# The quantised feed-forward layer at the end of an eight-sublayer transformer kernel, rewritten as one block and begun in the attention before it

## The chip, the core and the metric

The kernel runs on one core of one Trainium2 chip. The metric is the device time of one execution in microseconds (us); lower is better. TensorE is the matrix engine, VectorE (DVE), ScalarE (ACT) and GpSimd (POOL) are the three elementwise engines, SyncE (SP) issues the DMAs here.

## The reference

Activations x are 16 sequences of 256 tokens of 128 numbers, 4096 tokens in all, float32. Four pairs of sublayers follow, each `x = x + attention(layernorm(x))` and then `x = x + ffn(layernorm(x))`. The change is in the last feed-forward layer, with some of its work moved into the fourth attention (layer number 3, which the change's name calls the third). The last layer is this:

```python
def act_qdq(x):                      # 16 bits, one scale for the whole tensor
    scale = max(max(abs(x)) / 32767, 1e-12)
    return clip(round(x / scale), -32768, 32767) * scale
def fixed_qdq_u16(x):                # steps of 1/65536
    return clip(round(x * 65536), 0, 65535) / 65536
def lpbq_dequant(w): ...             # 4 bits, one scale for each block of 32 weights
x = act_qdq(x)
up = act_qdq(x @ lpbq_dequant(w_up).T)          # w_up, w_gate: 384 x 128
gate = act_qdq(x @ lpbq_dequant(w_gate).T)
gate = act_qdq(gate * fixed_qdq_u16(sigmoid(gate)))
o = act_qdq(gate * up)
return o @ lpbq_dequant(w_down).T
```

Each `act_qdq` needs the largest magnitude of a whole tensor before its first element can be quantised. So the layer is five passes over its data with a hard stop between each two: X (the normalised input), G (gate), U (up), GS (gate times its sigmoid) and O (the product).

## The kernel before

x stays in SBUF as `x_sb`, 128 partitions by 32 tiles of 128 numbers. Work goes in ITERS = 8 groups of four tiles, 512 tokens each. One program is written out for each engine and block, with named semaphores; an engine runs its list in order, and between two blocks all engines meet at a barrier. Nothing else sets the order.

**The attention before the last layer** (`narrow_attention`, layer 3, lines 608 to 1079) runs over b = 0 to 15. In step b VectorE adds the projection of sequence b-2, takes four row maxima of sequence b+1 (`largest`, L1012), and normalises the heads of sequence b-1 (`normalise`, L1019 and L1021), which TensorE projects in its next step. GpSimd adds biases and takes the roots of the layernorms; its last work is for group 7. The raw weights of the last layer (`wraw`, 128x1152) are loaded during this attention.

**The last layer** (`layer3_ffn`, L2136 to L2447) has five blocks.

1. *Normalise and transpose.* VectorE takes the statistics of all 32 tiles (L203), quantises the weights in seven steps over 128x1152 (L2230 to L2236) and normalises four tiles at a time (L2248), each followed by a row maximum (`largest`, L2240). GpSimd takes the roots (L232). TensorE transposes weights and x, ScalarE copies both out of PSUM.
2. *Project.* VectorE quantises a group of x (L2294, L2297), TensorE makes six 128x512 products (L2276; the trace counts two instructions for each float32 product), ScalarE copies them out (L2288), VectorE takes maxima over 1536 columns (L2302).
3. *Gate.* 24 rows of 512 columns go through ScalarE (L2338, L2340, L2345 the sigmoid), VectorE (L2354 to L2369) and a product on GpSimd (L2327), four rows deep.
4. *Product.* 24 rows: ScalarE L2387, VectorE L2395 and L2399.
5. *Down.* ScalarE L2428 and VectorE L2438 quantise a group of 1536 columns, TensorE multiplies it with the down weights (L2417), VectorE adds it to x (L2443).

At each of the five maxima `scale_vector` (L2175 to L2184) reduces to one column, GpSimd takes the maximum over partitions (L2188), and four short VectorE instructions make scale and inverse. After block 5 one DMA stores all of x (L2514).

Rounding is by adding and subtracting `MAGIC` = 1.5 * 2**23. On VectorE block 3 is this, for row r:

```python
nc.vector.tensor_scalar(gq[:, k, :], gq[:, k, :], -MAGIC, None, ALU.add)               # L2354
nc.vector.tensor_scalar(sg, sg, 65536.0, 65535.0, ALU.mult, ALU.min)                   # L2359
nc.vector.tensor_reduce(am[:, GS, bass.ds(r - 3, 1)], part(gtf, r - 3), ...)           # L2362
nc.vector.tensor_scalar(part(upf, r - 1), uq[:, (k - 1) % DEPTH, :], -MAGIC, None, ALU.add)
nc.vector.tensor_scalar(sg, sg, MAGIC, -MAGIC, ALU.add, ALU.add)                       # L2369
```

## Time and profile before

| | us |
|---|---|
| median of 3 runs | 1825.35 (1823.53 to 1826.36) |
| the profiled execution: device time | 1827.8 |
| its span, first to last instruction | 1826.0 |
| last layer, 1592.2 to 1826.0 | 233.8 |
| granted TensorE clock, mean | 0.924 of full speed |

The five blocks of the last layer begin at 1592.2, 1622.3, 1672.9, 1757.2 and 1789.4 us, and the last addition to x ends at 1819.06. A profile tells for each instruction its start, its length and what its engine waited for before it. The lengths of neighbours on one engine overlap by some 0.08 us, so that a row of equal instructions advances by a little less than the length of one. The granted clock is the share of 2.4 GHz that TensorE is given: 0.5 is 1.2 GHz.

### The profile page before, as it was taken

The numbers are of one execution on the slowest core, as the hardware profiler recorded it, in microseconds if no ns is written. First come the engines' busy times: TensorE is split into PE (matmuls) and PEld (weight loads), VectorE is DVE, ScalarE is ACT, GpSimd is POOL, SyncE is SP. The second block draws the span as 40 slices with busy tenths as digits, with TensorE's granted clock in tenths as the row PEclk, the third lists the DMA queues.
The fourth block names the chain that finished last, engine by engine and source line by source line (L and its number), as shares of the span: only waits on it lengthen the run. The fifth ranks groups of instructions, "written<-read, shape, count | busy, mean of one in ns | idle before, by whom it ended". The sixth has DMA issues, their size and how long they took to land. (4 is left out here: it accounts for less than half of the span.)

```text
span 1826.0 us, 25615 instructions
## 1 busy us (share of the span) xinstructions
PE 1502.6 (82%) x8105; PEld 1027.9 (56%) x8125; DVE 1257.8 (69%) x2784; ACT 886.6 (49%) x1622; POOL 201.7 (11%) x191
## 2 busy tenths in 40 slices
PE   6999988886999999889848999999999888665005
PEld 5777765554666666566536665666667455432005
DVE  3988965875677766566646666666665578677984
ACT  3666545773665555555513223322332267447742
POOL 2111012130000000211310000000000111011410
PEclk9999998997999999999969999999999999878557
DMA  4000003220000000332122234423443122000001
GB/s 164 1 1 0 1 1 97 68 53 1 1 1 1 0 0 1 99 102 57 29 93 116 112 120 162 162 107 124 162 162 133 56 60 53 19 0 0 0 0 46
DMA packets 32700, 108.01 MB, mean 59 GB/s; under 512 B 8845, under 2 KB 12301, under 8 KB 23502
## 3 DMA queue, kind: packets, MB, share of 16 engines
q1 hardware_dynamic: 32590, 106.64, 17.3%
q8 instruction: 57, 0.93, 0.2%
q14 instruction: 53, 0.43, 0.1%
HBM read 85.38 MB, written 2.36 MB: 48 GB/s over the span
## 5 line engine op out<-in xcount | busy, mean ns | idle before, releaser
L1012 DVE TENSOR_REDUCE mP_a<-psY_a 128x8 f32<-128x512 f32 x192 | 128.1, 688 | 101.1 <-PE psY_a L838 101.0
L756 ACT ACTIVATE probs_a<-psX_a 128x512 f32<-128x512 f32 x192 | 109.0, 595 | 125.1 <-PE psX_a L865 124.3
L1797 ACT ACTIVATE xsh_f<-xs_f 128x512 fp32r<-128x512 f32 x128 | 79.4, 630 | 166.9 <-DVE xs_f L2025 166.9
L2417 PE MATMUL ps_f<-wT_f,xq_f 128*128 128x128 f32 x192 | 26.0, 300 | 125.4 <-DVE xq_f L2438 125.3
L1555 DVE SCALAR_TENSOR_TENSOR g_f<-psU_f,cols_f1w,t_f 128x512 f32<-128x512 f32 (+1 forms) x104 | 78.0, 750 | 72.6 <-ACT t_f L1368 70.6
L1901 PE MATMUL psX_f<-xs_f,wo_f2w 128*128 128x512 f32 x256 | 121.3, 606 | 2.1 <-DVE xs_f L2025 1.5
L1368 ACT ACTIVATE t_f<-psU_f,cols_f1w 128x512 f32<-128x512 f32 (+1 forms) x104 | 71.2, 684 | 76.1 <-PE psU_f L1434 76.1
L1450 PE MATMUL psO_f<-h_f,w_f1w 128*128 128x512 f32 (+1 forms) x208 | 107.6, 599 | 0.0
L2029 DVE TENSOR_TENSOR xsl_f<-xs_f,xsh_f 128x512 fp32r<-128x512 f32 x128 | 87.9, 687 | 16.0 <-ACT xsh_f L1797 14.9
L838 PE MATMUL psY_a<-ks_a,xs_a 96*128 96x256 f32 x384 | 94.4, 347 | 4.1 <-DMA xs_a<-ql_a 2.5
L865 PE MATMUL psX_a<-xs_a,ks_a 128*128 128x256 f32 x384 | 86.1, 324 | 13.3 <-ACT xs_a L745 13.3
L2417 PEld LDWEIGHTS ps_f<-wT_f,xq_f 128*128 128x128 f32 x192 | 24.8, 212 | 127.2 <-issue 126.8
L1019 DVE RECIPROCAL heads_a<-psV_a 128x256 f32<-128x256 f32 x48 | 84.0, 1749 | 12.6 <-PE psV_a L878 12.6
L1913 PE MATMUL psQ_f<-xsh_f,wql_f2w 128*128 128x512 f32 x128 | 58.7, 459 | 35.2 <-DVE xsl_f L2029 34.8
L838 PEld LDWEIGHTS psY_a<-ks_a,xs_a 96*128 96x128 f32 x384 | 64.0, 198 | 33.9 <-DVE mP_a L1012 22.6
L182 POOL TENSOR_TENSOR rstd_f<-vareps_f,mhalf 128x4 f32<-128x4 f32 x16 | 18.1, 1133 | 562.0 <-DVE vareps_f L168 562.0
L1562 DVE TENSOR_TENSOR h_f<-act_h_f,psR_f 128x512 f32<-128x512 f32 (+1 forms) x104 | 70.6, 678 | 13.7 <-ACT act_h_f L1374 8.8
L865 PEld LDWEIGHTS psX_a<-xs_a,ks_a 128*128 128x128 f32 x384 | 63.3, 195 | 28.1 <-ACT xs_a L745 24.6
L1901 PEld LDWEIGHTS psX_f<-xs_f,wo_f2w 128*128 128x128 f32 x256 | 45.0, 192 | 48.9 <-issue 29.9
L1374 ACT ACTIVATE act_h_f<-g_f 128x512 f32<-128x512 f32 (+1 forms) x104 | 65.0, 625 | 3.2 <-DVE g_f L1555 3.0
L468 PE MATMUL psC_a<-vhat_a,pT_a 128*128 128x128 f32 x512 | 63.5, 278 | 0.5 <-DVE x_sb L545 0.5
L468 PEld LDWEIGHTS psC_a<-vhat_a,pT_a 128*128 128x128 f32 x512 | 61.5, 195 | 1.4 <-issue 0.6
(441 smaller groups left out, 4006.6 us busy)
## 6 DMA issues: line engine op xcount, KB each, us to landing
wq_f2w<-f_routes SPq DMA_DIRECT2D x16, 1024.0 KB, 4.7
wk_f2w<-f_routes SPq DMA_DIRECT2D x16, 1024.0 KB, 4.7
wv_f2w<-f_routes SPq DMA_DIRECT2D x16, 1024.0 KB, 4.6
ring_f2w<-f_routes SPq DMA_DIRECT2D x16, 1024.0 KB, 4.6
xs_a<-qh_a SPq DMA_DIRECT2D x168, 64.0 KB, 2.0
xs_a<-ql_a SPq DMA_DIRECT2D x84, 64.0 KB, 2.0
xs_a<-probs_a SPq DMA_DIRECT2D x36, 64.0 KB, 2.0
x_sb<-in_x SPq DMA_DIRECT2D x1, 2048.0 KB, 8.4
```

The source lines that it names most:

```text
L468: ins = nc.tensor.matmul(psC[:, 0:P], pT[:, g % 2, k * P:(k + 1) * P], vhat[:, g // TPI % 2, g % TPI // 2, k, :], start=k == 0, stop=k == ...
L756: nc.scalar.activation(probs[:, b % 2, g, :, :], psX[g % 2][:].rearrange("p (e t) -> p e t", e=2), ACT.Exp, scale=float(dv) ** -0.5).then_ ...
L838: ins = nc.tensor.matmul(psY[h % 2][:, e * GK:(e + 1) * GK], xs[0:MAXROW, j % 2, g, t:t + P], ks[0:MAXROW, j % 2, p, g, :], start=not mask ...
L865: ins = nc.tensor.matmul(psX[g % 2][:, e * ST:(e + 1) * ST], ks[:, j % 2, p, g, e * P:(e + 1) * P], xs[:, j % 2, g, p * ST:(p + 1) * ST], ...
L1012: nc.vector.tensor_reduce(mP[:, b % 2, h // 2, col:col + 8], psY[h % 2][:].rearrange("p (h k) -> p h k", h=8), axis=AX.X, op=ALU.max).then ...
L1019: nc.vector.reciprocal(heads[:, b % 2, :], psV[:, ST:2 * ST]).then_inc(s("sums_inverted").sem, 1)
L1368: nc.scalar.activation(t3[r, g % 2, :], psU[g % 2][r, 1, :], ACT.Identity, bias=cols[r, CH + g % CH:CH + g % CH + 1])\
L1450: ins = nc.tensor.matmul(psO[:], w2[0:rows[k], k, :], h[0:rows[k], g % 2, :], start=False, stop=k == CH - 1)
L1555: nc.vector.scalar_tensor_tensor(g_[r, g % 2, :], psU[g % 2][r, 0, :], cols[r, k:k + 1], t3[r, g % 2, :], ALU.add, ALU.mult).then_inc(s("h ...
L1797: nc.scalar.activation(xsh[:, e % RING, :], xs[:, e % RING, :], ACT.Copy).then_inc(s("x_high").sem, 1)
L1901: nc.tensor.matmul(psX[:], wo[:, e, :], xs[:, e % RING, :], start=e == 0, stop=e == E - 1)\
L2029: nc.vector.tensor_tensor(xsl[:, e % RING, :], xs[:, e % RING, :], xsh[:, e % RING, :], ALU.subtract)\
```

## The change

Work is moved out of block 1 into the attention's last steps: VectorE makes the weight scales at b = 11, the statistics of the first 16 tiles at b = 15 and their variances after that; GpSimd rounds the weights (four instructions over 1152 columns) and takes the roots for those 16 tiles. The five blocks become one, with no barrier inside. In it ScalarE normalises groups 0 to 3 and VectorE groups 4 to 7; TensorE runs filling matmuls (`keep_busy`) whose result nobody reads; the inverse of G is made as soon as the last gate maximum is there, ahead of the last maximum of U. Gate and product go in 8 operations of 1536 columns in place of 24 of 512. The sigmoid is clipped and rounded to 1/65536 by one instruction (adding 192), and a VectorE instruction takes 192 off and multiplies; GpSimd multiplies nothing. The rounding of up moves from VectorE to ScalarE. Each group of x is stored by a DMA of its own as soon as it is added to. The diff, cut to its core (project, down and the addition to x keep their instructions):

```diff
             ahead.split(pr, pool)
+            if layer == 3:
+                f3_weight_integers(pr, pool, ahead.tensors)
+                f3_rstd(pr, pool, common, ahead.tensors, 0)
...
                 if p and j + 2 < ITERS:
                     front_q(j + 2)
+                if layer == 3 and b == B - 5:
+                    dve.wait_ge(s("ahead").sem, s("ahead").at(16 * len(ahead.loads)))
+                    f3_weight_scales(pr, dve, ahead.tensors)
+                if layer == 3 and b == B - 1:
+                    f3_stats(pr, x_sb, ahead.tensors, range(HALF))
                 if b:
                     normalise(b - 1)
...
             add(B - 2)
+            if layer == 3:
+                f3_variances(pr, dve, Steps(dve, s("dve_steps"), ITERS, LN_STEPS), ahead.tensors, 0)
             normalise(B - 1)
             add(B - 1)
...
+def f3_weight_scales(pr, dve, t):
+    nc, done = pr.nc, pr.sig("w3_scales")
+    nc.vector.tensor_reduce(t["ws"][:], f3_blocks(t), axis=AX.X, op=ALU.max, apply_absolute_value=True).then_inc(done.sem, 1)
+    dve.wait_ge(done.sem, done.at(1))
+    nc.vector.tensor_scalar(t["ws"][:], t["ws"][:], 1.0 / 7.0, 1e-12, ALU.mult, ALU.max).then_inc(done.sem, 1)
+    dve.wait_ge(done.sem, done.at(2))
+    nc.vector.reciprocal(t["wi"][:], t["ws"][:]).then_inc(done.sem, 1)
...
+def f3_weight_integers(pr, pool, t):
+    nc, step = pr.nc, pr.sig("w3_steps")
+    wb = f3_blocks(t)
+    pool.wait_ge(pr.sig("w3_scales").sem, pr.sig("w3_scales").at(3))
+    nc.gpsimd.tensor_tensor(wb, wb, t["wi"][:].unsqueeze(2).broadcast_to(list(wb.shape)), ALU.mult).then_inc(step.sem, 1)
...
+    nc.gpsimd.tensor_scalar(t["wraw"][:], t["wraw"][:], MAGIC, -MAGIC, ALU.add, ALU.add).then_inc(step.sem, 1)
+    pool.wait_ge(step.sem, step.at(2))
+    nc.gpsimd.tensor_scalar(t["wraw"][:], t["wraw"][:], 7.0, -8.0, ALU.min, ALU.max).then_inc(step.sem, 1)
...
+def f3_rstd(pr, pool, w, t, half):
+    pool.wait_ge(pr.sig("var_half").sem, pr.sig("var_half").at(1))
+    for part in range(2):
+        a = half * HALF + part * HALF // 2
+        c = slice(a, a + HALF // 2)
+        pr.nc.gpsimd.tensor_tensor(t["rstd"][:, c], t["vareps"][:, c], w["mhalf"][:, 0:HALF // 2], ALU.pow)\
+            .then_inc(pr.sig("rstd_half").sem, 1)
...
+            @block.sync
+            def _(sp):
+                for i in range(ITERS):
+                    sp.wait_ge(s("x_added").sem, s("x_added").at(i + 1))
+                    sp.dma_start(out[:, i * TPI:(i + 1) * TPI, :], tile4(x_sb, i)).then_inc(s("out_stored").sem, 16)
...
+                nc.gpsimd.memset(magic[:], MAGIC).then_inc(s("pool_steps").sem, 1)
+                nc.gpsimd.memset(unmagic[:], -MAGIC).then_inc(s("pool_steps").sem, 1)
+                f3_rstd(pr, pool, common, wt, 1)
+                for n, k in enumerate((X, G, U, GS, O)):
+                    pool.wait_ge(s("absmax").sem, s("absmax").at(n + 1))
+                    nc.gpsimd.partition_all_reduce(gm[:, k:k + 1], amr[:, k:k + 1], P, bass.bass_isa.ReduceOp.max)\
...
+                def keep_busy(n):
+                    for _ in range(n):
+                        nc.tensor.matmul(PS[4][:], sel[:, 0, :], sel[:, 0:4, :], start=True, stop=True)
                 for k in range(3):
                     for j in range(NI):
                         ins = nc.tensor.transpose(PS[5 + k][:, j * P:(j + 1) * P], wraw[:, k, j * P:(j + 1) * P], ident[:])
                     ins.then_inc(s("vT").sem, 1)
+                keep_busy(8)
                 for i in range(ITERS):
-                    pe.wait_ge(s("ln_out").sem, s("ln_out").at(i + 1))
-                    pe.wait_ge(s("xT_ready").sem, s("xT_ready").at(i - 1))
+                    if i < ITERS // 2:
+                        pe.wait_ge(s("xn_act").sem, s("xn_act").at(i + 1))
+                    else:
+                        pe.wait_ge(s("xn_dve").sem, s("xn_dve").at(i + 1 - ITERS // 2))
+                    pe.wait_ge(s("xT_ready").sem, s("xT_ready").at(max(0, i - 3)))
                     for c in range(TPI):
-                        ins = nc.tensor.transpose(PS[i % 2][:, c * P:(c + 1) * P], xq[:, i % 2, 0, c * P:(c + 1) * P], ident[:])
+                        ins = nc.tensor.transpose(PS[i % 4][:, c * P:(c + 1) * P], xn(i)[:, c * P:(c + 1) * P], ident[:])
                     ins.then_inc(s("ln_T").sem, 1)
+                    keep_busy(12 if i == ITERS - 1 else 4)
...
+                pe.wait_ge(s("hidden_b").sem, s("hidden_b").at(ITERS * NP))
+                pe.wait_ge(s("o_made").sem, s("o_made").at(ITERS - 1))
+                keep_busy(28)
...
+                nc.scalar.activation(junk[:], magic[:], ACT.Sigmoid, scale=0.0)
+                def normalised(i):
+                    act.wait_ge(s("nb_ready").sem, s("nb_ready").at(1))
...
+                normalised(0)
+                normalised(1)
+                keep_x(0)
+                normalised(2)
+                keep_x(1)
+                normalised(3)
+                keep_x(2)
+                for k in range(3):
+                    keep_w(k)
+                for i in range(3, ITERS):
+                    keep_x(i)
...
+                scales(2)
+                gate_scaled(0)
+                gate_scaled(1)
+                for r in range(ITERS):
+                    sigmoid(r)
+                    if 1 <= r < ITERS - 1:
+                        gate_scaled(r + 1)
+                    up_scaled(r)
+                for r in range(3):
+                    up_int(r)
+                scales(4)
+                for r in range(ITERS):
+                    product_scaled(r)
+                    if r + 3 < ITERS:
+                        up_int(r + 3)
+                scales(5)
+                for r in range(ITERS):
+                    out_scaled(r)
...
+                nc.vector.scalar_tensor_tensor(nb[:], mean[:, 0:HALF], -1.0, rstd[:, 0:HALF], ALU.mult, ALU.mult)\
+                    .then_inc(s("nb_ready").sem, 1)
+                f3_stats(pr, x_sb, wt, range(HALF, TILES))
+                f3_variances(pr, dve, st, wt, 1)
+                for i in range(3):
+                    dve.wait_ge(s("xn_act").sem, s("xn_act").at(i + 1))
+                    largest(X, i, xn(i))
...
+                dve.wait_ge(s("maxed").sem, s("maxed").at(3 * ITERS - 1))
+                inverse(G, 2)
+                def gate_int(r):
+                    dve.wait_ge(s("scaled").sem, s("scaled").at(r + 1))
+                    nc.vector.tensor_scalar(qb[:, r % 2, :], qb[:, r % 2, :], -MAGIC, None, ALU.add).then_inc(s("gate_int").sem, 1)
+                def gated(r):
+                    dve.wait_ge(s("hidden_act").sem, s("hidden_act").at(r + 1))
+                    sg = sig[:, r % 2, :]
+                    nc.vector.tensor_scalar(sg, sg, 65535.0 / 65536.0, ROUND16, ALU.min, ALU.add).then_inc(s("hidden_ready").sem, 1)
+                    dve.wait_ge(s("hidden_ready").sem, s("hidden_ready").at(r + 1))
+                    nc.vector.scalar_tensor_tensor(gt[:, r, :], sg, -ROUND16, qb[:, r % 2, :], ALU.add, ALU.mult)\
+                        .then_inc(s("gated").sem, 1)
...
+                largest(U, ITERS - 1, up[:, ITERS - 1, :])
+                gate_int(0)
+                all_maxed(3)
+                inverse(U, 3)
+                for r in range(ITERS):
+                    gated(r)
+                    if r + 1 < ITERS:
+                        gate_int(r + 1)
+                    dve.wait_ge(s("gated").sem, s("gated").at(r + 1))
+                    largest(GS, r, gt[:, r, :])
+                all_maxed(4)
+                inverse(GS, 4, scale[:, G:G + 1])
...
+                def out_product(r):
+                    dve.wait_ge(s("gs_scaled").sem, s("gs_scaled").at(r + 1))
+                    dve.wait_ge(s("up_ready").sem, s("up_ready").at(r + 1))
+                    nc.vector.scalar_tensor_tensor(gt[:, r, :], gt[:, r, :], -MAGIC, up[:, r, :], ALU.add, ALU.mult)\
+                        .then_inc(s("o_made").sem, 1)
+                for r in range(ITERS):
+                    out_product(r)
+                    if r:
+                        dve.wait_ge(s("o_made").sem, s("o_made").at(r))
+                        largest(O, r - 1, gt[:, r - 1, :])
...
```

The order of instructions on VectorE in the attention, step b = 11. `heads_a` is what `normalise` makes, `x_sb` the addition. Before:

```order
L1004 SCALAR_TENSOR_TENSOR ql_a<-psF_a,cols_a3w,qh_a 128x512
L1019 RECIPROCAL heads_a<-psV_a 128x256
L1021 TENSOR_TENSOR heads_a<-psV_a,heads_a 128x256
L1028 TENSOR_TENSOR x_sb<-x_sb,psT_a 128x256
L1012 TENSOR_REDUCE mP_a<-psY_a 128x8 x4
```

And now:

```order
L1008 SCALAR_TENSOR_TENSOR ql_a<-psF_a,cols_a3w,qh_a 128x512
L2162 TENSOR_REDUCE ws_f3w<-wraw_f3w 128x36
L2164 TENSOR_SCALAR ws_f3w<-ws_f3w 128x36
L2166 RECIPROCAL wi_f3w<-ws_f3w 128x36
L1023 RECIPROCAL heads_a<-psV_a 128x256
L1025 TENSOR_TENSOR heads_a<-psV_a,heads_a 128x256
L1032 TENSOR_TENSOR x_sb<-x_sb,psT_a 128x256
L1016 TENSOR_REDUCE mP_a<-psY_a 128x8 x4
```

Three instructions of the weight scales stand between the query part of group 7 and the normalisation of sequence 10.

VectorE at the attention's end, from the addition of sequence 13. Before (the last three rows are normalisation and addition of sequence 15):

```order
L1028 TENSOR_TENSOR x_sb<-x_sb,psT_a 128x256
L1019 RECIPROCAL heads_a<-psV_a 128x256
L1021 TENSOR_TENSOR heads_a<-psV_a,heads_a 128x256
L1028 TENSOR_TENSOR x_sb<-x_sb,psT_a 128x256
L1019 RECIPROCAL heads_a<-psV_a 128x256
L1021 TENSOR_TENSOR heads_a<-psV_a,heads_a 128x256
L1028 TENSOR_TENSOR x_sb<-x_sb,psT_a 128x256
```

And now, from right behind that addition:

```order
L2185 BN_STATS stats_f3w<-x_sb 128x6 x16
L1023 RECIPROCAL heads_a<-psV_a 128x256
L1025 TENSOR_TENSOR heads_a<-psV_a,heads_a 128x256
L1032 TENSOR_TENSOR x_sb<-x_sb,psT_a 128x256
L2194 TENSOR_TENSOR mv_f3w<-stats_f3w 128x16
L2195 SCALAR_TENSOR_TENSOR mv_f3w<-stats_f3w 128x16
L2196 TENSOR_TENSOR mv_f3w<-stats_f3w 128x16
L2197 TENSOR_SCALAR mean_f3w<-mv_f3w 128x16
L2198 SCALAR_TENSOR_TENSOR mv_f3w<-mv_f3w 128x16
L2199 SCALAR_TENSOR_TENSOR vareps_f3w<-mv_f3w 128x16
L1023 RECIPROCAL heads_a<-psV_a 128x256
L1025 TENSOR_TENSOR heads_a<-psV_a,heads_a 128x256
```

Sixteen statistics stand ahead of the normalisation of sequence 14, six short instructions ahead of that of sequence 15.

VectorE in the gate pass, one round. Before, for one of 24 rows (address arithmetic left out):

```order
L2354 TENSOR_SCALAR xT_f<-xT_f 128x512
L2359 TENSOR_SCALAR xT_f<-xT_f 128x512
L2362 TENSOR_REDUCE am_f<-gt_f 128x1
L2366 TENSOR_SCALAR up_f<-xq_f 128x512
L2369 TENSOR_SCALAR xT_f<-xT_f 128x512
```

And now, for one of 8 (and the first of the next):

```order
L2474 TENSOR_SCALAR xT_f<-xT_f 128x1536
L2476 SCALAR_TENSOR_TENSOR gt_f<-xT_f,qb_f 128x1536
L2469 TENSOR_SCALAR qb_f<-qb_f 128x1536
L2412 TENSOR_REDUCE am_f<-gt_f 128x1
L2474 TENSOR_SCALAR xT_f<-xT_f 128x1536
```

A round has four instructions of 1536 columns where three rows had fifteen of 512.

## Rows read from the trace of the kernel before

**Rows 1.** busy time by stage of the last layer: stretch, length, five engines, TensorE clock, DMA
```profile
1592.00:1623.40 31.40, 9.71 (x41) 7.25 (x42) 28.62 (x93) 6.25 (x11) 8.15 (x7) 0.55 0.00 0
1623.40:1672.80 49.40, 43.49 (x96) 18.95 (x96) 35.14 (x40) 32.99 (x48) 0.70 (x2) 0.95 0.00 0
1672.80:1757.20 84.40, 0.00 (x0) 0.00 (x0) 72.71 (x126) 54.26 (x73) 31.80 (x25) 0.50 0.00 0
1757.20:1789.40 32.20, 0.00 (x0) 0.00 (x0) 29.93 (x54) 17.02 (x24) 0.35 (x1) 0.50 0.00 0
1789.40:1819.10 29.70, 25.96 (x192) 24.80 (x192) 13.69 (x16) 13.23 (x8) 0.00 (x0) 0.85 0.00 0
1819.10:1826.00 6.90, 0.00 (x0) 0.00 (x0) 0.00 (x0) 0.00 (x0) 0.00 (x0) 0.72 0.72 304
```

**Rows 2.** VectorE timeline, attention of layer 3: start, length, instruction, idle before it
```profile
1582.99 1.76 DVE L1019 RECIPROCAL heads_a<-psV_a 128x256 f32<-128x256 f32 x1 [3.21 <-PE psV_a L878]
...
1587.91 1.76 DVE L1019 RECIPROCAL heads_a<-psV_a 128x256 f32<-128x256 f32 x1 [1.47 <-PE psV_a L878]
```

**Rows 3.** VectorE timeline, last layer
```profile
1592.20 6.29 DVE L203 BATCH_NORM_STATS2 stats_f<-x_sb 128x6 f32<-128x128 f32 x32 [0.32 <-PEq L616]
...
1599.43 1.34 DVE L2230 TENSOR_REDUCE ws_f<-wraw_f3w 128x36 f32<-128x1152 f32 x1
...
1601.03 0.38 DVE L2232 RECIPROCAL wi_f<-ws_f 128x36 f32<-128x36 f32 x1
...
1605.70 2.14 DVE L2248 TENSOR_SCALAR xq_f<-x_sb,mean_f,rstd_f 128x128 f32<-128x128 f32 x8
...
1620.31 0.16 DVE L2178 TENSOR_REDUCE amr_f<-am_f 128x1 f32<-128x8 f32 x1
...
1712.72 1.52 DVE L2359 TENSOR_SCALAR xT_f<-xT_f 128x512 f32<-128x512 f32 x1
```

**Rows 4.** GpSimd timeline, last layer
```profile
1599.67 7.61 POOL L232 TENSOR_TENSOR rstd_f<-vareps_f,mhalf_f 128x8 f32<-128x8 f32 x4 [7.35 <-DVE vareps_f L212]
...
1755.30 0.38 POOL L2188 PARTITION_ALL_REDUCE gm_f<-amr_f  x1 [5.98 <-issue]
```

**Rows 5.** groups by line of the last 286 us: instruction, count, busy us, mean ns
```profile
L2438 DVE TENSOR_SCALAR xq_f<-xq_f 128x1536 f32<-128x1536 f32 x8 | 7.7, 960 | 8.5 <-ACT xq_f L2428 8.5
...
L2302 DVE TENSOR_REDUCE am_f<-gt_f (+1 forms) x8 | 14.0, 1752 | 6.3 <-ACT gt_f L2288 6.0 <-issue 0.2
...
L2395 DVE SCALAR_TENSOR_TENSOR gt_f<-gt_f,up_f (+1 forms) x24 | 16.4, 684 | 1.5 <-ACT gt_f L2387 1.5
...
L2428 ACT ACTIVATE xq_f<-gt_f,magic_f,inv_f 128x1536 f32 x8 | 13.2, 1666 | 26.7 <-PEq L2379 15.2 <-PE ps_f L2417 11.6
...
L2338 ACT ACTIVATE xT_f<-gt_f,magic_f,inv_f 128x512 f32 (+1 forms) x24 | 19.5, 811 | 16.1 <-POOL gt_f L2327 10.8 <-PEq L2261 5.2
...
L2345 ACT ACTIVATE xT_f<-xT_f,scale_f 128x512 f32<-128x512 f32 x24 | 17.3, 720 | 5.8 <-DVE xT_f L2354 5.8
...
L2276 PE MATMUL ps_f<-xq_f,wT_f 128*128 128x512 f32 x96 | 43.5, 616 | 3.1 <-DVE xq_f L2297 3.1
```

**Rows 6.** GpSimd groups by form, whole span
```profile
L139 POOL TENSOR_TENSOR wkl_f2w<-wk_f2w,wkh_f2w 128x2048 fp32r<-128x2048 f32 x1 | 4.6, 4628 | 0.1
```

**Rows 7.** TensorE timeline, filling matmuls at the start of the attention of layer 3
```profile
1455.82 2.09 PE L892 MATMUL psV_a<-sel 128*128 128x512 f32 x8
```

**Rows 8.** ScalarE timeline, a copy out of PSUM in the projection
```profile
1641.26 0.69 ACT L2288 ACTIVATE up_f<-ps_f,scale_f 128x512 f32 x1 [0.17 <-PE ps_f L2276]
```

**Rows 9.** chain of waits of the last layer: start, length, what
```profile
1792.20 11.36 PE ps_f L2417 x72
...
1803.59 5.84 PE ps_f L2417 x48
```

**Rows 10.** DMA issues: KB each, median us from issue to landing
```profile
out<-x_sb SPq DMA_DIRECT2D x1, 2048.0 KB, 6.3
...
xs_a<-qh_a SPq DMA_DIRECT2D x168, 64.0 KB, 2.0
```

446 lines of the change are left out of this document (194 added, 252 removed).

## The prediction

> **What bounds the kernel now.** I read the granted clock by stage first, then the timelines of VectorE, ScalarE, GpSimd and TensorE over the last layer, then the groups by line for the price of each form. The chain of waits covers only the final block, so it doesn't help ahead of 1789 us. The change touches nothing before 1554 us; all of it happens in the last 270 us.
>
> The six stages of the last layer show who is busy [rows 1]: in the first 31.4 us VectorE for 28.6; in the projection TensorE for 43.5 of 49.4; in the gate pass VectorE for 72.7 of 84.4; in the product pass VectorE for 29.9 of 32.2; in the down pass TensorE for 26.0 of 29.7; then 6.9 us for the store. So it is VectorE, TensorE, VectorE, VectorE, TensorE, DMA, and each is followed by a stop.
>
> The gate pass costs VectorE 3.03 us a row, 72.7 us for 24. Of that, 1.44 us is one clipping instruction over 512 columns, listed at 1.52 us [rows 3]; its neighbours of the same kind and size take 0.41. It starts 0.07 us behind a GpSimd product of 1.31 us, and ends with it. The products cost VectorE 1.1 us in each row.
>
> **The change part by part.** All times of the new block are counted from its start t = 0, which is 1592.2 us of before. Prices of 1536 columns: VectorE's subtraction 0.96 us, its maximum 1.75, ScalarE's quantisation 1.67 [rows 5]. The two-operand instruction is 0.684 for 512 [rows 5], so for 1536 it is 1.75 by the slope of the maximum. The sigmoid is 0.72 for 512 [rows 5]; with ScalarE's slope of (1.666 - 0.811) / 1024 a column it is 1.57. Behind each other without a wait they advance by some 0.08 less on VectorE (1.67, 0.88) and 0.11 less on ScalarE (1.55).
>
> *Attention.* The weight scales are three dependent instructions, from 1599.43 to 1601.41 [rows 3], 2.0 us. In step b = 11 VectorE has nothing to cover them: its waits in a step are of 0.5 to 0.8 us for TensorE, and TensorE waits for VectorE's heads in the same step. Between no delay and 2.0 us I take 2.0. The 16 statistics are half of 6.29 [rows 3], 3.15 us, and stand where VectorE waited 3.21; the six short instructions, 0.9 us, stand where it waited 1.47 [rows 2]. Both cost nothing; without that cover they would cost 4.0. GpSimd's four weight instructions: at 4.63 us for 2048 columns [rows 6] one of 1152 takes 2.6, all four 10.4, from about 1557 to 1567 us, and the next work for GpSimd is at 1587.
>
> *Normalisation.* Before, TensorE began the projection 31.2 us behind the block's start. Now VectorE is through statistics and variances at t = 4.3, GpSimd's two roots end at 8.2 (7.61 for four [rows 4]). ScalarE loads its table (the 1.28 us before the first sigmoid, in the timeline), and normalises 4 x 128 columns at 0.40 each by the slope above, 1.6 us a group. TensorE turns the weights (9 transposes, 2.2 us) and fills: eight matmuls at 0.43 at half clock, up to 5.7. From then a group costs it 0.55 for four transposes and 4 x 0.24 (seven steps of (2.09 - 0.39) / 7 [rows 7]), 1.5. The first copy of x ends at 6.7, ScalarE's groups 2 and 3 at 8.3 and 10.5, VectorE's third maximum at 8.9, its group 4 at 10.0. Behind 10.5 VectorE alternates 1.1 (eight normalisations in 2.14 [rows 3]) and 0.6, up to the last maximum at 16.7. The scale takes 1.4 (1620.31 to 1621.75), the first group of quantised x 0.9: 19.0. TensorE has turned the last group at 16.8 and fills twelve times, to 19.6, which is later. Saved: 31.2 - 19.6 = **11.6**.
>
> *Projection.* 48 products; the pitch at full clock is 0.86 (a copy of 0.69 and a wait of 0.17 for the next product [rows 8]), 41.3 us against 43.5 [rows 5]. The clock was 0.95 in that stage and half at its start [rows 1]; with TensorE filling right up to it I take all of the difference: **2.2**. It ends at t = 60.9.
>
> *From the last product to the gate pass.* Before: 6.0 us (1666.9 to 1672.86), with two maxima, two scales and a barrier. Now the scale of G follows the last gate maximum, which ends 0.1 ahead of TensorE's end, so 1.4 later: t = 62.3, saved **4.6**. The last maximum of U and its scale run beside ScalarE's first two quantisations.
>
> *Gate pass.* VectorE has 0.88 + 1.67 + 0.88 + 1.67 = 5.1 a round. The chain of one round is clip and round 0.99, product 1.67, integers 0.99, sigmoid 1.61: 5.26. ScalarE has 1.55 + 1.55 + 1.57 = 4.7, so the chain decides. The first sigmoid ends at t = 67.1, eight rounds less the one missing subtraction end at 108.2, the scale at 109.7. That is 47.4 us against 83.7 (the 84.4 of [rows 1] less a barrier): **36.3**. In the 83.7 is a wait of 5.98 us by GpSimd ahead of the maximum over partitions [rows 4]; here it has nothing else to do and 0.55 us is enough, as at the first. ScalarE with its three first roundings of up is 0.3 late; the barrier of 0.67 goes: **0.4**.
>
> *Product pass.* Eight times 1.67 + 1.67, plus the first 1.7 and the scale 1.7: 30.2 against 31.45, **1.2**, and its barrier **0.7**. It ends at t = 140.2.
>
> *Down.* The first 36 products of 96 ran at half clock: 11.36 us, where the next 24 took 5.84, 2.92 for twelve [rows 9]. 28 filling matmuls start at t = 133.5 and take 8.5 to 9.3, the first at half clock, and the first group is ready at 142.9. So eight groups at 2.92: 26.9 from the stop to the last addition, against 29.65: **2.8**.
>
> *Store.* 2048 KB land in 6.3 us and 64 KB in 2.0 [rows 10], so 256 KB between; along the line 2.4. All but the last are covered. 6.9 becomes 3.1: **3.9** (bounds 0 and 4.4).
>
> Sum: 11.6 + 2.2 + 4.6 + 36.3 + 0.4 + 1.2 + 0.7 + 2.8 + 3.9 - 2.0 = 61.7. The profiled execution took 1827.8, so 1766.1; the median of the runs is 2.45 lower, which gives **1763.7**.
>
> GpSimd runs its maximum over partitions behind other work, and the trace shows what that can cost: the 5.98 us of [rows 4] come right behind its last product. At the first maximum, 1620.61, it answered in 0.14 us, 13.3 us behind its last root. Now this gap is from 8.2 to 16.9, 8.7 us, more than 5.98, so I add nothing. The Trainium skill (GPSIMD Engine Reference, 2.1 Instruction dispatch) says that the first call to freshly loaded code pays about 6 us with nothing shown. By that rule, too, the load would end at 14.2 if it begins behind the last root, and the sum stays; if it began with the call, the sum would lose 6.
>
> **The rivals.**
> 1. *TensorE stays at half clock in the normalisation.* For: it was at 0.55 there [rows 1], and it starts the block behind idle stretches. Against: 9 transposes and 8 fillings stand in one piece, and the projection reached full clock after some 4 us of unbroken work. At half clock a group costs 0.9 + 1.7 = 2.6; the last transposes end at 24.8, the fillings at 30, and nothing of 11.6 and 2.2 is left but 1.2: 1776.
> 2. *GpSimd's 5.98 us is exposed at the first maximum*, because the gap counts from the request. Against: the answer at 1620.61. 1769.7.
> 3. *A round of the gate pass is longer*, since clip, product and sigmoid wait for each other and an answer between engines may take more than the 0.04 I gave. At 6.0 us a round: 1769.6. On the other side, the weight scales may be absorbed and the product pass may start on time: 1761.
> 4. *Slower: GpSimd's rounding of the weights outlasts the attention.* The price per column in this trace is 2.3 ns for a subtraction [rows 6] but 240 ns for a root (7.61 us for 32 columns [rows 4]). From 7.5 us for each of the four instructions it delays the roots of the first half and with them the block; from 23 us each (20 ns a column) the kernel is slower than before. At the root's price it would be some 1100 us for the four: 2840. Multiplications, additions and minima are next to the subtraction and not to the root, so I give it little.
> 5. *The change doesn't do what it says*: the filling matmuls may not raise the clock for the down pass, 2.8 us: 1766.5.
>
> **How the numbers follow.** The sum as forecast 0.62 (1763.7); rival 1: 0.12; rival 2: 0.06; rival 3 with its other side 0.12; rival 5: 0.05; rival 4: 0.03, of which 0.01 is slower. The range takes in rivals 1 to 3 and 5 and, below, the bounds of scales (2.0), normalisation (ScalarE's 128 columns at 0.3, 1.5) and gate rounds at 5.1 (1.3), with as much again for what I didn't see: 1756 to 1777. The likeliest case alone is 1760 to 1768. Some 0.2%, 3.7 us, is what a measurement tells from no change. Faster 0.98, same 0.01, slower 0.01.
>
> **What would show it.** Right: the new block starts near 1594; the projection's first product some 20 us later at clock 1.0; rounds of the gate pass every 5.3 us; VectorE's clip at 0.96 us; passes of 30 and 27 us; the last DMA landing within 2.5 us. Wrong: the granted clock at 0.5 ahead of the projection (rival 1), GpSimd issuing its first maximum late (rival 2), idle VectorE in the gate pass (rival 3), or an attention that ends at 1600 or later (rival 4).

## The result and the profile after

The change takes the kernel from 1824.44 us (median of 4 runs, 1821.03 to 1826.36) to **1770.03 us** (median of 4, 1768.6 to 1771.26). The ratio is 0.9703, with a 95% interval of 0.9687 to 0.972: about 54 us, 3% faster. The profiled execution took 1769.78 us with a span of 1767.8 (before: 1827.8 and 1826.0), at a mean granted clock of 0.945 (before 0.924). The forecast was 1763.7, with 61.7 us less from one profiled execution to the other; their spans differ by 58.2.

Busy time by stage of the changed last layer, with the columns of [rows 1]: normalisation, projection, gate, product, down, store.

```profile
1597.10:1615.30 18.20, 17.72 (x90) 14.30 (x90) 15.11 (x55) 13.19 (x29) 3.74 (x5) 0.91 0.01 1
1615.30:1658.10 42.80, 41.42 (x97) 18.11 (x96) 32.35 (x35) 32.98 (x48) 0.35 (x1) 1.00 0.00 1
1658.10:1705.80 47.70, 0.00 (x0) 0.00 (x0) 45.33 (x43) 41.94 (x27) 0.70 (x2) 0.51 0.00 0
1705.80:1737.40 31.60, 8.27 (x27) 6.64 (x28) 27.90 (x23) 19.91 (x14) 0.35 (x1) 0.56 0.00 0
1737.40:1765.30 27.90, 24.71 (x195) 23.53 (x193) 13.67 (x16) 13.22 (x8) 0.00 (x0) 0.94 0.18 66
1765.30:1767.80 2.50, 0.00 (x0) 0.00 (x0) 0.02 (x1) 0.00 (x0) 0.00 (x0) 1.00 0.28 105
```

The first column against [rows 1] shows where the time went: 31.4 to 18.2, 49.4 to 42.8, 84.4 to 47.7. VectorE is busy for 45.3 of 47.7 us of the gate pass, where it was busy for 72.7 of 84.4: it is still hardly ever idle there, with the work done in fewer, wider instructions. In the granted clock (the third figure from the end) the normalisation went from 0.55 to 0.91 and the down pass from 0.85 to 0.94.

One round of the gate pass, VectorE's timeline (start, length, instruction):

```profile
1662.89 0.96 DVE L2474 TENSOR_SCALAR xT_f<-xT_f 128x1536 f32<-128x1536 f32 x1 [0.86 <-ACT xT_f L2354]
1663.89 1.76 DVE L2476 SCALAR_TENSOR_TENSOR gt_f<-xT_f,qb_f 128x1536 f32<-128x1536 f32 x1
1665.57 0.95 DVE L2469 TENSOR_SCALAR qb_f<-qb_f 128x1536 f32<-128x1536 f32 x1
1666.44 1.75 DVE L2412 TENSOR_REDUCE am_f<-gt_f 128x1 f32<-128x1536 f32 x1
1668.16 0.96 DVE L2474 TENSOR_SCALAR xT_f<-xT_f 128x1536 f32<-128x1536 f32 x1
```

From clip to clip it is 5.27 us, without an idle gap behind the first: 5.26 had been forecast. The sigmoid that the next clip needs, in ScalarE's timeline:

```profile
1666.56 1.57 ACT L2354 ACTIVATE xT_f<-qb_f,scale_f 128x1536 f32<-128x1536 f32 x1 [2.20 <-DVE qb_f L2469]
```

It ends at 1668.13 and the clip starts at 1668.16. VectorE alone would have come to that clip at 1668.11 (its maximum starts at 1666.44 and lets the next instruction start 1.67 later). So the chain through both engines sets the pace, as forecast, but VectorE's own work, 5.2 us a round, is only some 0.05 us behind it.

What didn't go as forecast is the attention ahead of the block. I measure it from the start of GpSimd's last bias addition (1542.56 before, 1543.23 after) to the end of VectorE's last addition (1591.88 and 1596.81): the **stretch** of all that follows. It is 49.32 us before and 53.58 after, 4.3 us longer where 2.0 had been forecast. VectorE's and TensorE's timelines around the weight scales, after:

```profile
1554.76 0.74 DVE L1008 SCALAR_TENSOR_TENSOR ql_a<-psF_a,cols_a3w,qh_a 128x512 fp32r<-128x512 f32 x1
1555.42 1.34 DVE L2162 TENSOR_REDUCE ws_f3w<-wraw_f3w 128x36 f32<-128x1152 f32 x1
...
1557.31 1.70 DVE L1023 RECIPROCAL heads_a<-psV_a 128x256 f32<-128x256 f32 x1
```

```profile
1559.52 0.99 PE L891 MATMUL psT_a<-ws_a3w,heads_a 128*128 128x128 f32 x4 [2.12 <-DVE heads_a L1025]
...
1561.72 1.79 PE L882 MATMUL psV_a<-probs_a,vs_a 128*32 128x256 f32 x16
```

And the stretches of 2 us there:

```profile
1558.00:1560.00 2.00, 0.48 (x3) 0.48 (x4) 1.43 (x2) 0.75 (x2) 1.68 (x2) 0.95 0.42 107
1560.00:1562.00 2.00, 2.00 (x13) 1.70 (x15) 1.45 (x3) 0.17 (x1) 2.00 (x1) 0.50 0.44 112
1562.00:1564.00 2.00, 2.00 (x22) 0.82 (x18) 0.29 (x2) 2.00 (x4) 2.00 (x1) 0.69 0.43 107
```

The scales put VectorE's head division off from 1555.42 to 1557.31. TensorE, which wants the heads, stands idle for 2.12 us, and right behind that the granted clock is 0.50: its sixteen products for the next heads take 1.79 us, where they take 1.07 at full clock. So there are two costs: VectorE's own time, which I had counted, and a step at half clock, which I had not. One trace could show a chance fall of the clock. But the same step, to b = 11 in the table below, took 8.57 to 9.93 us in all six traces that have the scales in one piece and nothing filled ahead of it (this one and five of the runs below), and 7.19 to 7.21 in the three that have no scales at all.

The distances between the starts of VectorE's head divisions, one for each sequence, tell it step by step. The last column is from the last division to the end of the stretch, and all are worked out from the rows of those divisions.

| | to b=10 | 11 | 12 | 13 | 14 | 15 | end | stretch |
|---|---|---|---|---|---|---|---|---|
| before | 7.86 | 7.20 | 7.20 | 7.20 | 6.64 | 4.92 | 3.97 | 49.32 |
| after | 9.75 | 8.71 | 7.20 | 7.20 | 6.73 | 6.21 | 3.45 | 53.58 |

That is +1.89 for the scales, +1.51 for the step at half clock, and +0.86 in the last three columns. The statistics and variances there stood where VectorE had waited, as forecast: the wait of 3.21 us in [rows 2] is 0.20 after.

```profile
1583.77 3.18 DVE L2185 BATCH_NORM_STATS2 stats_f3w<-x_sb 128x6 f32<-128x128 f32 x16
1587.15 1.76 DVE L1023 RECIPROCAL heads_a<-psV_a 128x256 f32<-128x256 f32 x1 [0.20 <-PE psV_a L882]
```

But the clock of 1590 to 1592 us is 0.63 and of 1592 to 1594 it is 0.51, in the middle of TensorE's last heads.

GpSimd's rounding of the weights and its maxima over partitions, GpSimd's timeline after:

```profile
1557.47 2.13 POOL L2174 TENSOR_TENSOR wraw_f3w<-wraw_f3w,wi_f3w 128x1152 f32<-128x1152 f32 x1 [12.97 <-DVE wi_f3w L2166]
1559.92 4.13 POOL L2176 TENSOR_SCALAR wraw_f3w<-wraw_f3w 128x1152 f32<-128x1152 f32 x1 [0.32 <-POOL wraw_f3w L2174]
1564.14 1.15 POOL L2178 TENSOR_SCALAR wraw_f3w<-wraw_f3w 128x1152 f32<-128x1152 f32 x1
1565.37 2.13 POOL L2180 TENSOR_TENSOR wraw_f3w<-wraw_f3w,ws_f3w 128x1152 f32<-128x1152 f32 x1
...
1601.76 3.23 POOL L2209 TENSOR_TENSOR rstd_f3w<-vareps_f3w,mhalf 128x8 f32<-128x8 f32 x2 [4.54 <-DVE vareps_f3w L2199]
1612.89 0.38 POOL L2260 PARTITION_ALL_REDUCE gm_f<-amr_f  x1 [7.90 <-DVE amr_f L2402]
...
1704.59 0.35 POOL L2260 PARTITION_ALL_REDUCE gm_f<-amr_f  x1 [43.31 <-DVE amr_f L2402]
```

The rounding ends at 1567.5. The first maximum over partitions starts 0.14 us behind its input (1612.75), and none of them is held up: the 5.98 us of [rows 4] are gone.

The entry into the down pass, TensorE's timeline, then two pieces of the chain of waits:

```profile
1729.13 8.85 PE L2268 MATMUL ps_f<-sel 128*128 128x512 f32 x28 [72.41 <-DVE gt_f L2495]
1740.18 24.35 PE L2301 MATMUL ps_f<-wT_f,qb_f 128*128 128x128 f32 x192 [2.20 <-DVE qb_f L2510]
```

```profile
1740.18 4.59 PE ps_f L2301 x24
...
1747.51 2.96 PE ps_f L2301 x24
```

The filling ends at 1737.98, 2.2 us before the first product may begin, and the first 24 products take 4.59 us in place of 2.96. The store, in the list of DMA issues (KB each, median us to landing):

```profile
out<-x_sb SPq DMA_DIRECT2D x8, 256.0 KB, 2.0
```

### The profile page after: what moved, and what is told of

The parts are those of the page before. It is cut to its first block and busy times, and to the rows that moved or that the text cites. A ratio compares the mean times of both kernels' runs of the same rounds, so it can differ in the third digit from the quotient of the medians.

```text
span 1767.8 us, 24778 instructions
## 1 busy us (share of the span) xinstructions
PE 1516.7 (86%) x8181; PEld 1038.8 (59%) x8201; DVE 1217.6 (69%) x2650; ACT 883.5 (50%) x1583; POOL 178.4 (10%) x171
## 5 line engine op out<-in xcount | busy, mean ns | idle before, releaser
L2268 PE MATMUL ps_f<-sel 128*128 128x512 f32 x76 | 23.1, 452 | 72.4 <-DVE gt_f L2495 72.4
L2268 PEld LDWEIGHTS ps_f<-sel 128*128 128x128 f32 x76 | 15.9, 221 | 76.4 <-issue 73.2
```

## The experiments

Times of whole executions of one kernel lie 2 to 16 us apart, and some 6 us of that arise ahead of the change (last section). So each run is read by its trace, of which there is one for each kernel: by the stretch defined above, and by the pieces of the block behind it, counted from the end of the last addition. In the profiled run of the changed kernel these are: 18.5 to the first projection product, 41.4 projection, 83.5 to the first down product, 25.1 to the last addition, 2.5 to the end, 171.0 in all. Where nothing was changed in a piece or just ahead of it, it agreed within 0.3 us from run to run, with one exception that is told below. The first piece answers to what stands just ahead of it: it is 19.0 us in the run without weight work and 17.8 in the four runs that fill the attention's tail. Each ratio in brackets is to executions of the kernel before that were measured beside that run, with medians of 1824.3 to 1827.0 us.

### The weight work in the attention

**No weight work** leaves out the weights' scales and their rounding; the layer then works with the raw weights.

```diff
-                    f3_weight_scales(pr, dve, ahead.tensors)
...
-                f3_weight_integers(pr, pool, ahead.tensors)
```

> The changed kernel without any preparation of the last layer's weights (no scales on VectorE, no rounding on GpSimd; the layer multiplies with the raw weights). Measure: from the start of GpSimd's last bias addition to the end of the attention's last addition, 49.3 us before and 53.6 in the changed kernel, 4.3 longer. Theory C (clock): the three scale instructions hold VectorE for 2.0 us, TensorE idles 2.1 for it, its clock falls to half and its next work takes 1.4 longer, 3.4 in all; 0.9 more is the clock at the attention's end. Then this stretch is 3.4 shorter, 50.2, and the kernel some 3.4 us faster, 1766.6. Theory G (GpSimd): the 1.4 comes from GpSimd working beside the attention. Then it is 50.2 here too: only the next run tells the two apart. Rival D: the 3.4 is not from the scales at all: 53.6.

Measured: 1765.47 us (ratio 0.9654, 0.9623 to 0.9685). The stretch is 49.33 us, within 0.01 of the kernel before, with all steps as before (7.86, 7.19, 7.20, 7.20, 6.67, 4.91, 3.97). TensorE's products for the heads follow after a wait of 0.28 us where it was 2.12:

```profile
1555.27 0.71 PE L890 MATMUL psT_a<-ws_a3w,heads_a 128*128 128x128 f32 x4 [0.28 <-DVE heads_a L1024]
```

So the whole 4.3 us hangs on the weight work. The 16 statistics, the six short instructions for the variances and the two roots, all still there, cost nothing in the attention, as forecast. The tail's extra 0.9 is gone too, though no work was taken from the tail. That isn't this trace alone: the last three columns of the table add up to 15.2 to 15.6 us in the three traces without the scales (before, this run, the products on VectorE) and to 16.4 to 17.5 in the six with them and an unfilled tail. By which way work at b = 11 lengthens the tail is open.

**No rounding** leaves GpSimd's four instructions out and keeps VectorE's scales; the weights are not rounded.

```diff
-                f3_weight_integers(pr, pool, ahead.tensors)
```

> The changed kernel without GpSimd's four instructions on the weights (the scales stay on VectorE but are not used; the layer multiplies with the raw weights). Theory C: nothing changes, the stretch stays at 53.6 us, TensorE's clock falls behind the scales as before, 1770. Theory G: the stretch is 1.4 shorter, 52.2, and the kernel 1768.6.

Measured: 1768.09 us (0.9683, 0.9634 to 0.9733); stretch 53.69, steps 9.75, 8.70, ..., 6.27, 3.46. That is the changed kernel again: GpSimd's 10 us of rounding cost nothing, and rival 4 has no share in the result.

**Scales split** makes the scales in five pieces, in steps 8 to 12, where VectorE waits for TensorE.

```diff
+                if layer == 3 and B - 8 <= b <= B - 4:
+                    ...
+                    f3_scale_part(pr, dve, ahead.tensors, b - (B - 8))
...
-                if layer == 3 and b == B - 5:
-                    ...
-                    f3_weight_scales(pr, dve, ahead.tensors)
```

> The weight scales in five pieces (three maxima over 12 blocks each, 0.5 us, and the two short instructions), one at the head of each of steps 8 to 12 of the attention, where VectorE waits 0.8 us for TensorE's projection. Theory C: TensorE never idles 2 us, the clock stays at 1.0, and nearly all of 3.4 us comes back: stretch 50.2 to 50.7, kernel 1766.6 to 1767.1. If every piece still costs its own length (2.2 us in all) but the clock holds: 52.4 and 1768.8.

Measured: 1765.95 us (0.966, 0.9628 to 0.9692); stretch 52.85. The first two steps are back at 7.86 and 7.20, so the pieces cost VectorE nothing. Yet the next is 8.73, and the last three columns are 6.44, 7.12 and 3.97. The gain that I expected was eaten by two other steps at half clock (0.50 at 1560 to 1562 us of this trace and from 1580 to 1588). Which clock a step gets is not set by VectorE's work in it alone. A filling can show whether it can be set.

### Filling TensorE's idle time in the attention

**Tail filling** adds products of 512 columns that nobody reads, 5, 7 and 8 of them, at three places of the third attention's tail, to the changed kernel (`fill(n)` issues n of them).

```diff
+                if not more:
+                    fill(5)
                 scores_T(b, 0)
...
+            fill(7)
             project(B - 2)
...
             for part in range(2):
                 heads_out(B - 1, part)
+            fill(8)
```

> The changed kernel with products that compute nothing in front of the last three waits of TensorE in the third attention (5, 7 and 8 of them, 512 wide). Output the same. Theory A: the attention's tail is longer than before because the clock is at half there: from the start of the second last but one head division to the last addition 9.7 us now, 8.9 before. With the filling the clock stays at full and it is 8.9 or less, -0.8. Theory B: it is longer because VectorE does statistics and variances in front of the heads there, and the filling changes nothing or adds 0.5 for the time that it holds TensorE. The 3.4 us at the weight scales stay in both.

Measured: 1764.39 us (0.9676, 0.9633 to 0.9719); stretch 51.89. The steps are 9.75, 8.60, 7.20, 7.20, 6.45, 4.90, 3.45, so the tail is 1.3 us shorter than in the changed kernel (8.35 from the division of b=14, 9.66 there), and 0.5 shorter than before the change. The granted clock of the tail, which was 0.63 and 0.51 in the changed kernel's last heads, stays at 1.00 (stretches of this run):

```profile
1584.00:1586.00 2.00, 0.76 (x8) 0.64 (x12) 1.16 (x3) 0.00 (x0) 0.00 (x0) 1.00 0.00 0
1586.00:1588.00 2.00, 2.00 (x33) 1.07 (x32) 1.25 (x8) 0.00 (x0) 0.72 (x1) 1.00 0.00 0
```

This is theory A, with more than its 0.8; that VectorE's statistics lengthen the tail, theory B, is out. The full clock also lasts into the block: the granted clock of its first 4 us is 1.00, where it was 0.57 in the changed kernel, the first eight fillings take 2.08 us in place of 3.02, and the first projection product comes 0.7 us earlier. One piece of the block was longer here, though nothing in it was changed: the 28 fillings took 8.15 us and ended 2.9 us ahead of the first down product, the clock stood at 0.50 for most of the first 5 us of products, and the piece took 26.3 in place of 25.1.

**Step filling alone** keeps the scales in one piece and adds three products ahead of `scores_T(b, 0)` in steps 8 to 14, besides those of the tail.

```diff
+                if B - 8 <= b:
+                    fill(3 if more else 5)
                 scores_T(b, 0)
```

> The changed kernel with its weight scales in one piece, and the products of nothing in steps 8 to 15 and at the tail; 28 in front of the down pass. Output the same. It parts the 3.4 us at the weight scales: theory A: 1.9 is VectorE's own time, 1.5 a step at half clock behind it, caused by TensorE's idle 2.1 us; the three products fill part of that gap, the step is 7.2 to 7.5 in place of 8.7, and the stretch 51.0 to 51.5 us. Theory B: they come too early in the step to fill the gap in which TensorE waits for the heads, the clock falls as before, and the stretch is 51.9 as with the tail filling alone.

Measured: 1764.92 us (0.967, 0.9643 to 0.9698); stretch 50.59. The step with the scales is still 9.75 long, but the next is 7.15, and TensorE's wait for the heads is 1.42 us, after which the same four products take 0.71 and not 0.99:

```profile
1557.89 0.71 PE L891 MATMUL psT_a<-ws_a3w,heads_a 128*128 128x128 f32 x4 [1.42 <-DVE heads_a L1033]
```

That parts the 3.4 us: 1.9 is VectorE's own time, 1.5 the half clock, which three products of 0.7 us take away. It is one trace with the filling against six without it, in each of which the step is 8.57 us or more.

**Split and tail filling**, with 36 fillings ahead of the down pass as well: scales split, the tail filling, `keep_busy(36)` for `keep_busy(28)`.

> The changed kernel with the weight scales of VectorE in five pieces over steps 8 to 12 of the third attention, 36 products of nothing in front of the down pass in place of 28, and the products of nothing at the attention's tail. Output the same. It repeats the first two thirds of the run with the split scales, in which the pieces cost VectorE no time of their own (the head divisions came at 12.19 and 19.39 us behind the bias addition, as before the change) and yet one step then ran at half clock (8.73 us in place of 7.20). Theory A: that fall of the clock was chance, since the rows of TensorE were the same in the run without the weight work, whose clock held; then it may be gone here, and the stretch from the bias addition to the attention's last addition is 48.8 to 49.3 us. Theory B: it belongs to what the weight work does on other engines (GpSimd's 10 us), the step takes 8.6 to 8.8 again, and the stretch is 50.3 to 50.8. The block behind it takes 169.1 (as with 36 products) in both. The changed kernel has 53.6 and 171.0.

Measured: **1759.56 us** (0.9641, 0.962 to 0.9663). Stretch 48.58, block 168.6: by its trace the attention is now 0.7 us shorter than before the change. The steps are 7.85, 7.20, 7.20, 7.20, 6.45, 4.90 and 3.45. The half-clock step of the split scales is gone although nothing is filled there. The same place in the two traces, first scales split, then this run:

```profile
1558.00:1560.00 2.00, 1.97 (x12) 1.81 (x12) 1.19 (x3) 1.17 (x2) 1.83 (x3) 0.81 0.00 0
1560.00:1562.00 2.00, 2.00 (x18) 0.65 (x17) 0.85 (x2) 0.60 (x1) 1.62 (x1) 0.50 0.04 8
```

```profile
1564.00:1566.00 2.00, 1.93 (x16) 1.64 (x20) 1.16 (x4) 1.20 (x4) 1.83 (x3) 1.00 0.00 0
1566.00:1568.00 2.00, 2.00 (x33) 1.01 (x31) 1.47 (x3) 0.58 (x1) 1.66 (x1) 1.00 0.03 8
```

Both follow 2 us in which TensorE was busy for 0.5, with GpSimd rounding in both. One falls to half clock, the other stays. GpSimd's work alone, theory B, does not decide it; the fall comes and goes with the same instructions. So the 48.58 us are in part luck. Of the 5.0 us below the changed kernel, 1.6 are the filled tail, 1.9 VectorE's time that the split hides, and 1.5 a step at full clock that nothing in this kernel secures.

**Split, tail and step filling** has all of them.

> As the split and tail filling, and in addition 3 products of nothing ahead of the first transposed scores of each of the steps 8 to 14, where TensorE waits 0.8 to 1.2 us for ScalarE's maxima. Output the same. Theory A (mine): TensorE has so little to do in these steps that its clock stands at the edge, and the three products, 0.7 us, keep it at full: no step over 7.9, the stretch 48.9 to 49.5 us, against 53.6 in the changed kernel; with the 36 products in front of the down pass the block is 169.1 in place of 171.0. Together some 6 us below the changed kernel by the trace, 1764 or less by the median. Rival: the products hold TensorE beyond its wait and every step grows by up to 0.5, 3.5 us in all, or they don't keep the clock, and the stretch is 50 to 53.

Measured: 1762.33 us (0.9657, 0.9634 to 0.968). Stretch 48.88, block 168.6; steps 7.86, 7.34, 7.20, 7.20, 6.45, 4.89, 3.46. The step filling costs 0.3 us where it is not needed. Of this and the run above, each has beaten the kernel before and the changed one, whose interval begins at 0.9687. The medians of the two stand 2.8 apart, but with overlapping intervals and by their traces within 0.3.

### The block

**More filling**: 36 products in front of the down pass, nothing else.

```diff
-                keep_busy(28)
+                keep_busy(36)
```

> 36 in place of 28 filling matmuls ahead of the down pass. In the changed kernel the 28 end 2.2 us ahead of the first product, the clock falls, and the first twelve products take 4.6 us where later ones take 2.9. Theory C: eight more at 0.24 fill 1.9 of the 2.2 us, the clock stays up, the first group takes 2.9 to 3.0, and the kernel is 1.4 to 1.6 us faster, 1768.5. If the fall comes from something else (the gap of the steps, not its length), the first group stays at 4.6 and the time at 1770.

Measured: 1772.84 us (0.9699, 0.9662 to 0.9736). The four executions lie at 1767.5, 1769.3, 1776.4 and 1776.6, so the median can't show a gain of 1.6. By the trace the piece from the first down product to the last addition is 23.5 us against 25.1. The filling now ends 0.64 us ahead of the first product, and the first 24 take 2.96 us (chain of waits of this run):

```profile
1739.62 2.96 PE ps_f L2301 x24
```

**No filling**: `keep_busy` in the last block issues nothing.

```diff
-                    for _ in range(n):
+                    for _ in range(0):
```

> The changed kernel without the matrix products of the last layer that compute nothing and are there for TensorE's clock: those in the normalisation and the 28 in front of the down pass. Its output is the same. Theory (mine): they carry two of my terms. Without them TensorE enters the projection at half clock, so the 18.5 us between the attention's last addition and the first projection product grow by 0 to 2 (VectorE and ScalarE set that pace) and the projection itself by 1 to 2 over 41.4; the down pass begins at half clock for its first 24 products and more (4.6 us now, 5.9 then), +1 to +1.5 against 25.1. Sum +3 to +5. Rival: the clock is full in the projection within its first few products anyway, and what is left of the filling's worth is the down pass alone, +1.3 or less; or the products of nothing delay the transposes behind them, and the normalisation gets shorter, -0.5. The measured time moves with what the attentions before do (the start of the last bias addition of GpSimd lay between 1536.8 and 1543.2 us in five traces), so the stretches of the trace decide.

Measured: 1769.33 us (0.9695, 0.9661 to 0.9729). The block is 173.2 against 171.0: the first projection product comes 0.7 us earlier (17.8), the projection takes 1.4 more (42.9), the down piece 1.2 more (26.4). The stretches of normalisation, the projection's first 4 us and the down pass's first 6 us:

```profile
1596.20:1612.10 15.90, 9.04 (x35) 6.08 (x34) 13.87 (x49) 11.48 (x27) 3.62 (x3) 0.50 0.00 0
1612.10:1616.10 4.00, 3.99 (x6) 1.84 (x7) 0.58 (x2) 1.24 (x2) 0.00 (x0) 0.63 0.00 0
...
1738.60:1744.60 6.00, 5.96 (x28) 5.99 (x29) 1.42 (x2) 0.74 (x2) 0.00 (x0) 0.50 0.01 3
```

All fillings of the block together are worth 2.2 us, not the 3 to 5 expected. TensorE is busy for 9.0 of the 15.9 us of the first row, at half clock: VectorE and ScalarE set the pace of the normalisation, and the fillings, which run at half clock at first, held the first projection product up. With a full clock from the tail filling they don't: 17.8 us there too, with all fillings in place. This run also had the longest stretch of all, 56.4 us, with an attention whose code is the changed kernel's: steps 9.75, 9.93, 8.55, 7.20, 6.82, 6.37, 3.46. Its median hides that, and the loss of the filling with it, because its second attention was 6.2 us shorter (128.5 us against 134.7, last section).

**One store** replaces the eight transfers by one behind the last addition.

```diff
-                for i in range(ITERS):
-                    sp.wait_ge(s("x_added").sem, s("x_added").at(i + 1))
-                    sp.dma_start(out[:, i * TPI:(i + 1) * TPI, :], tile4(x_sb, i)).then_inc(s("out_stored").sem, 16)
+                sp.wait_ge(s("x_added").sem, s("x_added").at(ITERS))
+                sp.dma_start(out, x_sb[:]).then_inc(s("out_stored").sem, 16)
```

> The changed kernel with the output stored by one transfer behind the last addition, as before, in place of eight. Theory (mine): the last addition to the end takes 6.5 to 6.9 us in place of 2.5, as rows 10 and 1 have it, so +4.0 to +4.4 us on the block. Rival: the long end before was due to what else the queues carried there and not to the size, and one transfer costs 3 to 4 us, so +1 or less.

Measured: 1772.79 us (0.9718, 0.9683 to 0.9753). From the last addition to the end 6.76 us against 2.48, +4.3, all else as in the changed kernel. The one transfer of 2048 KB lands in 6.3 us, as it did before the change.

**The products to VectorE** is the kernel before with one part of the change alone (VectorE makes each product one row later than GpSimd did).

```diff
-                        nc.gpsimd.tensor_tensor(part(gtf, r - 1), gq[:, (k - 1) % DEPTH, :], sig[:, (k - 1) % DEPTH, :], ALU.mult)\
-                            .then_inc(s("hidden_mul").sem, 1)
...
+                        dve.wait_ge(s("hidden_ready").sem, s("hidden_ready").at(r - 1))
+                        nc.vector.tensor_tensor(part(gtf, r - 2), gq[:, (k - 2) % DEPTH, :], sig[:, (k - 2) % DEPTH, :], ALU.mult)\
+                            .then_inc(s("hidden_mul").sem, 1)
```

> The kernel before with one part of the change alone: the 24 products sig(g) * g of 512 columns in each sweep of the gate pass are VectorE's, GpSimd does none; everything else is as before (512 columns an instruction, 24 rows in each pass). Theory (mine): GpSimd's product held VectorE's clipping up from 0.41 to 1.52 us in each row, so VectorE gains 1.1 and takes over a product of 0.68 less the overlap of 0.08, net 0.5 a row, 12 us in the gate pass of 84; with GpSimd's exposed 5.98 us gone at its start as well, 12 to 17 of the 36.3 us that I put on this pass. The rest, 20 to 24, is then the width of 1536. Rival: the two engines did not disturb each other, the 1.52 us is the instruction's own, and VectorE loses 0.6 a row, 14 us slower.

Measured: 1809.55 us (ratio to the kernel before 0.9925, 0.9898 to 0.9952). One row of the gate pass, VectorE's timeline of this run:

```profile
1697.29 0.43 DVE L2353 TENSOR_SCALAR xT_f<-xT_f 128x512 f32<-128x512 f32 x1
1697.62 0.69 DVE L2356 TENSOR_TENSOR gt_f<-xT_f 128x512 f32 x1
1698.23 0.69 DVE L2360 TENSOR_REDUCE am_f<-gt_f  x1
...
1699.49 0.43 DVE L2348 TENSOR_SCALAR xT_f<-xT_f 128x512 f32<-128x512 f32 x1
```

The clip that took 1.52 us [rows 3] takes 0.43 with GpSimd idle, and a row takes 2.54 us where it took 3.03. The kernel before shows the same within its own pass: its last clip had no product beside it and took 0.41, and two instructions later the subtraction of up, else 0.41, ran into GpSimd's product (1746.02 to 1747.31 us) and took 0.91.

```profile
1745.76 0.41 DVE L2359 TENSOR_SCALAR xT_f<-xT_f 128x512 f32<-128x512 f32 x1
1746.09 0.68 DVE L2362 TENSOR_REDUCE am_f<-gt_f 128x1 f32<-128x512 f32 x1
1746.69 0.91 DVE L2366 TENSOR_SCALAR up_f<-xq_f 128x512 f32<-128x512 f32 x1
```

From the previous maximum over partitions to that of GS it is 68.3 us (1668.82 to 1737.16) against 84.1 (1671.19 to 1755.30), **15.8 less**. Of that, 11.8 are 24 rows; the maximum over partitions now starts 0.09 us behind its input, where it took 4.9, and 0.8 of the two is lost at the pass's ends. The change made the pass 36.6 us shorter, and 15.8 come from taking GpSimd off it. The other 21 are what is left over for the width of 1536, the clip and rounding in one instruction, and up's rounding on ScalarE; these three weren't told apart.

## Why the prediction came out as it did

Step by step between the two profiled executions, with the saving forecast and the saving measured:

| step of the prediction | forecast | measured | where |
|---|---|---|---|
| normalisation | 11.6 | 13.0 | 31.2 to 18.2 |
| projection | 2.2 | 2.1 | 43.5 to 41.4 |
| last product to gate pass | 4.6 | 4.6 | 6.0 to 1.36 |
| gate pass, ScalarE late, barrier | 36.7 | 36.6 | 84.34 to 47.76 |
| product pass, barrier | 1.9 | 0.7 | 32.2 to 31.5 |
| down | 2.8 | 1.7 | 29.66 to 27.97 |
| store | 3.9 | 4.5 | 6.94 to 2.48 |
| attention | -2.0 | -4.3 | 49.3 to 53.6 |
| ahead of the change | 0 | -0.7 | |
| sum | 61.7 | 58.2 | |

(The last column's block pieces end at the scales: G at 1658.06, GS at 1705.82, O at 1737.35 us.)

**The main mechanism was right**: the gate pass is bound by the chain of clip, product, integers and sigmoid, and GpSimd's product was what held VectorE's clip. The products-to-VectorE run shows the second half of that by itself. The chain is longer than VectorE's own work by only 0.05 us a round, and not by the 0.16 forecast (5.26 against 5.1): VectorE's clip and product follow each other after 1.00 us and not 0.88, since the second waits for the first. One reading was loose: the clip did not end with GpSimd's product but 0.28 us behind it (1714.24 and 1713.96). Rival 3 didn't come: a round is 5.27 us. The normalisation, with its work moved into the attention, and the other half of the gate pass have no experiment of their own: there the traces agree with the sum, which does not show the cause.

**The step that failed** is "Between no delay and 2.0 us I take 2.0", in the attention. The 2.0 was right as VectorE's own time (1.89), but it was priced as if TensorE only waited. TensorE waited 2.12 us, and its next step ran at half clock: +1.5, shown by the step filling, which removes just this. The tail's +0.9 is of the same kind: the tail filling takes it away, and 0.5 more. Why the tail's clock fell with the scales in place and not without them is open. My bound from above was no bound: a delay on VectorE can cost more than itself through the clock of the engine that waits.

**Down** missed by 1.1 because the 28 fillings were forecast to end at 142.0 to 142.8 us of the block, with the first group ready at 142.9. They started at 132.0 and not at 133.5, took 8.85, and ended at 140.9; the first product came at 143.1, behind 2.2 us of idleness, and within a microsecond the clock was at 0.50. 36 fillings give 1.6 back.

**Product pass**: I charged one start of 1.7 us ahead of the eight rounds. VectorE waits twice, because it has no maximum to make between the first and the second product:

```profile
1707.62 1.76 DVE L2495 SCALAR_TENSOR_TENSOR gt_f<-gt_f,up_f 128x1536 f32<-128x1536 f32 x1 [1.79 <-ACT gt_f L2368]
1710.58 1.76 DVE L2495 SCALAR_TENSOR_TENSOR gt_f<-gt_f,up_f 128x1536 f32<-128x1536 f32 x1 [1.21 <-ACT gt_f L2368]
```

The 1.21 is the whole miss.

**Normalisation** was better by 1.4: ScalarE was through its fourth group at 9.3 us of the block, not at 10.5, and TensorE through the weights and the first eight fillings at 4.7, not 5.7; the last group was turned at 15.5 and not 16.8.

**Rival 1**, half clock in the normalisation, came for the first 4 us of the block only (0.57, then 1.00; 0.91 in all). Most of its 12.4 us was the price of the fillings themselves at half clock throughout, which no run shows; half clock without them made the normalisation 0.7 shorter and the projection 1.4 longer, and with the down pass cost 2.2 in the whole block. **Rival 5** came in part: the fillings raised the clock for the down pass, but not up to its first product. **Rival 2** did not come: the row at 1612.89 waits for its input, with 7.90 us behind GpSimd's last root. By the Trainium skill (GPSIMD Engine Reference, 2.1 Instruction dispatch) a first call to freshly loaded code pays about 6 us. The traces agree in part: [rows 4] has 5.98 us right behind a product, and the gaps of 7.9 us and more ahead of a maximum over partitions show none. The other way round it is less clear. At the start of the gate pass before, GpSimd's first product came 8.98 us behind a maximum over partitions and still 1.6 us behind its input, the rounding below, and what held it is open:

```profile
1678.53 0.42 DVE L2369 TENSOR_SCALAR xT_f<-xT_f 128x512 f32<-128x512 f32 x1
...
1680.52 1.28 POOL L2327 TENSOR_TENSOR gt_f<-xT_f 128x512 f32<-128x512 f32 x1 [8.98 <-issue]
```

No run here had a gap shorter than 7.9 us between a root and a maximum, so the case in between is not shown.

**From the profiled execution to the median** I lost another 2.7 us. The profiled run of the kernel before was 2.45 us above its median and I took that off; that of the changed kernel is 0.25 below its own. Between the profiled executions the forecast missed by 3.7 (1766.1 against 1769.8), of which 3.5 are in the table and 0.2 outside the span. Together that is the distance from 1763.7 to 1770.0. The 2.7 are scatter between executions. The 3.5 would be more without luck: the normalisation and the store came out 1.4 and 0.6 us better than forecast, which hid part of what the attention, the product pass and the down pass missed.

## What to carry to other kernels

Work put on an engine "in its wait" is free only up to that wait; beyond it, count also what the engine that is kept waiting loses in clock. Cut such work into pieces and lay one into each wait, and give TensorE something to do in its own long waits: here five pieces and twenty products that nobody reads turned +4.3 us into -0.7 in one trace. The pieces alone left it at +3.5 in another, because two steps fell to half clock. An elementwise product that is handed to GpSimd to relieve VectorE can cost VectorE more than doing it; look whether some VectorE instruction in the same loop is longer than its neighbours of the same shape.

## What the runs showed of the hardware beyond that

**The clock of a step comes and goes with the same code.** In the second attention (layer 1), untouched by any of these kernels, four steps, the second, fourth, sixth and eighth, take 10.38 or 11.9 us each. The same step in the kernel before and in the run with scales split:

```profile
807.40:819.30 11.90, 9.88 (x69) 6.14 (x67) 7.67 (x21) 5.21 (x9) 1.14 (x1) 0.86 0.09 24
```

```profile
808.00:818.30 10.30, 8.36 (x69) 5.21 (x67) 7.51 (x20) 5.15 (x9) 1.14 (x1) 1.00 0.11 31
```

TensorE does the same 69 instructions, once at a mean clock of 0.86 and once at 1.00. From the first head division of this attention to its last it was 134.6 to 134.7 us in five of the thirteen traces (before, changed, more filling, one store, split with step filling), 133.3 in one, 130.1 in two and 128.5 in five. Some 6 us of an execution are decided there, which is why a difference of 2 or 3 us between medians of this kernel says little where the trace says much. What decides it isn't shown by any row; it stays open. A filling as in the third attention was not tried there.

**One GpSimd TENSOR_SCALAR is dear**: the one that adds and subtracts `MAGIC` took 4.13 us for 1152 columns in all nine traces that have it, where the one behind it, of the same size, took 1.15, while a TENSOR_TENSOR of that size took 2.13. The two differ in their operations (additions; minimum and maximum) and in that one is the first of its kind, and no run tells which of these it is. It was hidden here, as the run without rounding shows.

**GpSimd disturbs VectorE only in some of its work.** Its product of 512 columns stretched a VectorE clip from 0.41 to 1.52 us, and at other places the subtraction of up (0.91) and the rounding (1.53 at 1680.56 us), but not VectorE's maximum over 512 columns, which took 0.68 beside it (1746.09). Its roots (3.29 us for two) ran beside one of VectorE's head divisions and its rounding beside another, and these took 1.76 and 1.70 us, as elsewhere; those read PSUM. The Trainium skill (SBUF — State Buffer, SBUF: two separate sides) tells of an exclusive lock on one pair of ports, for which a GpSimd instruction and some forms of VectorE's stand in line, the later one blocked for the whole of the other. The traces agree for the clip and the subtraction, which both ended some 0.3 us behind GpSimd's product; no VectorE instruction of 512 columns or more between two places of SBUF runs beside GpSimd's rounding, so there it is not tested.
